# State steps of layer 2: half of the output sum on TensorE, and a new order of rows, experts and softplus parts

## The chip, the cores and the metric

The kernel runs on one core of a Trainium2 chip. The metric is the device time of one execution in microseconds (us). Every time below is in us unless ns is written.

## The reference, cut to what matters

The program is a network of four layers on activations of B = 4 batches, S = 512 positions and D = 128 channels. The change lies in layer 2, which has two parts that work on the same input.

The first is a selective state-space scan with 256 inner channels and 16 states. For every batch the normed input goes through an input projection, a convolution of width 3 and silu, which give x; small products of x give a step size dt (through softplus), and the rows B and C. For every state n of 16 the layer then computes

```
h_t = exp(dt_t * A_n) * h_(t-1) + dt_t * x_t * B_t[n]      (over the 512 positions)
y_t = sum over n of h_t * C_t[n]   (+ D_param * x_t)
```

The sum y is multiplied by silu(z), goes through an output projection, is added to the normed input and normed again.

The second part is a mixture of 8 experts with 512 hidden units each, of which the router chooses two for each position. The silu of its sum gates the first part's result.

## The kernel before, in words

The 256 inner channels lie as two halves m = 0, 1 of 128 partitions each, with the 512 positions along the free axis. A **state step** k (0 to 63) is one state n = k % 16 of one batch b = k // 16; the text says "step 7" for n = 7 of any batch. All five engines run hand-ordered lists of these steps, each in its own `@block`, and signal each other by semaphores. For one step:

- VectorE (loop at L2116 and on): `scan(k)` (L2042) runs the recurrence over 1024 elements; `outs(k-1)` (L2050) multiplies the states of the step before by the row C, one instruction per half; `inputs(k+2)` (L2035) makes dt * x * B for two steps ahead; in even steps `add_expert` (L2066) adds one expert's output, four instructions.
- TensorE (loop at L1814): two `chunk`s (each 4 products of hidden units with `we2`, 16 instructions for both), then `c_row(k)` (the row C of state k copied onto 128 partitions, bank 2; it waits for `outs(k-1)`), two `hidden`s (a 128x128 product of 512 columns each), then `b_row(k+3)` (the row B, bank 1; it waits for `inputs(k+2)`). A product of fp32 operands shows as two instructions; the rows, which are in another type, as one. All matrix products have line L415, a helper's.
- ScalarE (loop at L1952): in even steps the decays exp(dt * A) of two steps (L1915), in odd steps four silus of hidden units (L1903). It loads an activation table each time that it changes between the two.
- GpSimd: `add_y(k)` (L1681) adds the two halves of `outs(k)` to the sum YY (L1693); at a batch's first state it sets each half of YY to D_param * x before (L1689).

H, the buffer of states, has four slots, so `inputs(k)` waits until `add_y(k-4)` is through.

Into these steps the rest of a batch is laid, by hand. The products that use bank 0 ("spares", `spare_at`, L1610 to L1625) are written by TensorE in a fixed order and each waits until the one before is read: the experts' biases in step 1, the output projection `wo` of the batch before in step 3, and for the batch to come the transposes in step 4, the router in 5 and its logits in 6, the convolution `c` (two halves, six instructions each) in 7, `dbc` in 8, `dt` in 9, the transposed weights in 14; `z` in 12 and 13. The first spare of a step stands right behind `c_row`, further ones behind the `hidden`s.

VectorE reads some of them: `biases` (L2055) in step 2, behind `inputs`; `out_stats` (L2080) in step 3, `choose` (L1989 and on) in step 6, `split` (L2006) in step 9, all behind `inputs`. The softplus of the next batch's dt is spread: ScalarE's `dt_parts` in step 9, `dt_exp` (L1876) and `dt_log` (L1882) in step 10; VectorE's `correction` (L2013) in step 10, `share` (L1999) and `dt_sums` (L2020) in step 11, `dt_x` (L2027) in step 13. `gated` (L2073, sum times silu(z)) comes in step 1 of the next batch behind `scan`; ScalarE's `gate` (L1896) comes at the end of its step 1, and `finish` (L2092 and on) in VectorE's step 5.

Of the kernel before, what the change touches and what calls it, by code (L numbers as in the profile page):

```python
# [20 lines left out]
ALU = mybir.AluOpType  # L21
# [3 lines left out]
P = 128  # L25
# [8 lines left out]
def build(nc, I, out):  # L34
    ctx = ExitStack()
    with ctx:
# [1548 lines left out]
        def layer2():  # L1585
# [6 lines left out]
            bm, ex, scn, hc, ya = (lsem(f"a2_{k}") for k in ("inputs", "decays", "scans", "outs", "y"))  # L1592
# [37 lines left out]
            with ExitStack() as c:  # L1630
# [5 lines left out]
                YY = sbr("YY", [P, 2, S], c=c)  # L1636
# [19 lines left out]
                with nc.Block() as block:  # L1656
# [5 lines left out]
                    def _(g):  # L1662
# [18 lines left out]
                        def add_y(k):  # L1681
                            b, n = divmod(k, NS)
                            if n == 0:
                                g.wait_ge(m0, read("c", b, 1))
                                if b:
                                    g.wait_ge(yz, b)
                            for m in range(2):
                                if n == 0:
                                    plink(nc.gpsimd.tensor_scalar(YY[:, m, :], XM[:, m, :], Dp[:, m:m + 1], None, ALU.mult))  # L1689
                                else:  # L1690
                                    g.wait_ge(ya, 2 * k + m - 1)
                                g.wait_ge(hc, 2 * k + m + 1)
                                nc.gpsimd.tensor_tensor(YY[:, m, :], YY[:, m, :], H[:, k % 4, m, :], ALU.add).then_inc(ya, 1)  # L1693

                        nc.gpsimd.memset(XT[:, :, 0:1], 0.0)
                        nc.gpsimd.memset(XT[:, :, S + 1:S + 2], 0.0).then_inc(zd, 1)
                        nc.gpsimd.memset(BCR[0:32, :, :].bitcast(F32), 0.0).then_inc(zd, 1)
                        scales(0)
# [13 lines left out]
                    def _(pe):  # L1712
                        def spare(key):
# [32 lines left out]
                            elif kind == "bias":  # L1746
                                for t in range(T):
                                    last = mm(o[:, t * P:(t + 1) * P], WGT[0:NE, t * P:(t + 1) * P], be2f[0:NE, :])
                            elif kind == "z":
                                last = mm(o, WinT[:, 2 + key[2], :], xt)  # L1750
                            elif kind == "wo":
                                pe.wait_ge(yz, b + 1)
                                for t in range(T):
                                    for m in range(2):
                                        last = mm(o[:, t * P:(t + 1) * P], ZS[:, m, t * P:(t + 1) * P], WoutT[:, m, :],
                                                  start=m == 0, stop=m == 1)
# [11 lines left out]
                        def chunk(g):  # L1768
# [3 lines left out]
                            if i == 0 and j >= 2:  # L1772
                                pe.wait_ge(ad, j - 1)
                            for t in range(T):
                                last = mm(PS[:, 6 + j % 2, t * P:(t + 1) * P], HH[:, i, t * P:(t + 1) * P],
# [14 lines left out]
                        def c_row(k):  # L1790
                            b, n = divmod(k, NS)
                            if k:
                                pe.wait_ge(hc, 2 * k)
                            mm(PS[:, 2, :], SEL[:, NS + n:NS + n + 1].to_broadcast([96, P]), BCR[:, b % 2, :]).then_inc(cp, 1)

# [18 lines left out]
                        for k in range(NK):  # L1814
                            for i in range(2):
                                chunk(2 * k + i)
                            if k:
                                c_row(k)
                            for key in spare_at[k][:1]:
# [6 lines left out]
                            if k + 3 < NK:  # L1826
                                b_row(k + 3)
# [3 lines left out]
                    def _(act):  # L1831
# [24 lines left out]
                        def x_silu(b, m):  # L1856
                            act.wait_ge(mp, read("c", b, m))
                            if b:
                                act.wait_ge(ya, 2 * NS * (b - 1) + 2)
# [20 lines left out]
                        def dt_log(b):  # L1880
                            act.wait_ge(cor, b + 1)
                            nc.scalar.activation(E, E, ACT.Ln, bias=1.0).then_inc(dtl, 1)  # L1882

# [21 lines left out]
                        def decays(k):  # L1905
# [3 lines left out]
                            if k == 0:  # L1909
                                act.wait_ge(wj, 2)  # L1910
                                act.wait_ge(zd, 3)
# [19 lines left out]
                        dt_log(0)  # L1931
                        decays(0)
                        decays(1)
                        store_wT(0)
                        for k in range(NK):
# [14 lines left out]
                            if n == 1 and b:  # L1950
                                gate(b - 1)
                            if n == 3 and more:  # L1952
# [13 lines left out]
                            if n == 10 and more:  # L1966
                                dt_exp(b + 1)
                                dt_log(b + 1)
# [8 lines left out]
                    def _(v):  # L1977
# [51 lines left out]
                        def inputs(k):  # L2029
# [3 lines left out]
                            if k >= 4:  # L2033
                                v.wait_ge(ya, 2 * (k - 3))
# [10 lines left out]
                        def outs(k):  # L2045
                            v.wait_ge(cp, k + 1)
                            v.wait_ge(scn, k + 1)
                            for m in range(2):
                                h = H[:, k % 4, m, :]
                                nc.vector.tensor_tensor(h, h, PS[:, 2, :], ALU.mult).then_inc(hc, 1)  # L2050
# [7 lines left out]
                        def add_expert(j):  # L2058
# [6 lines left out]
                            for t in range(T):  # L2065
                                last = nc.vector.scalar_tensor_tensor(ACC[:, t, :], PS[:, 6 + j % 2, t * P:(t + 1) * P],  # L2066
# [3 lines left out]
                        def gated(b):  # L2070
                            v.wait_ge(m0, read("z", b, 1))
                            v.wait_ge(ya, 2 * NS * (b + 1))
                            nc.vector.tensor_tensor(ZS, ZS, YY[:, :, :], ALU.mult).then_inc(yz, 1)  # L2073
# [39 lines left out]
                        for k in range(NK):  # L2113
# [3 lines left out]
                            if n == 1 and b:  # L2117
                                gated(b - 1)
                            if k:
# [5 lines left out]
                            if n == 2:  # L2125
                                biases(b)
                            if n % 2 == 0 and k:
                                add_expert(k // 2 - 1)
# [8 lines left out]
                            if n == 10 and more:  # L2137
                                correction(b + 1)
                            if n == 11 and more:
                                share(b + 1)  # L2140
                                dt_sums(b + 1)
# [749 lines left out]
```

## Time and profile before

| what | us |
| --- | --- |
| median of 3 runs (lowest, highest) | 1602.43 (1601.49, 1605.38) |
| the profiled execution's own time | 1599.87 |
| its span, first to last instruction | 1596.9 |
| layer 2's state steps, first to last scan start | 893.6 to 1331.0 |
| busy over the span: TensorE, VectorE, ScalarE, GpSimd | 1243.1, 1031.2, 736.3, 617.0 |
| mean granted share of TensorE's clock | 0.891 |

The page divides the span among engines (PE is TensorE, PEld its weight loads, DVE VectorE, ACT ScalarE, POOL GpSimd). The shares are means over layers with different limits, so for this change the views are restricted to 893 to 1335 us, the state steps. A row's last part in square brackets, or behind the last bar, is the idle time of the engine in front of the instruction and the instruction that ended it. PEclk is the granted share of TensorE's clock, 1.00 for 2.4 GHz and 0.5 for 1.2 GHz.

### The profile page before, as it was taken

The page shows a single profiled execution, that of the slowest core. Times are in us where ns is not written, and L with a number is a line of the kernel's source. Part 1 is how long each engine was busy: PE and PEld are TensorE (multiplying, and loading weights), DVE is VectorE, ACT ScalarE, POOL GpSimd, SP SyncE. Part 2 cuts the span into 40 slices and gives each one's busy share as a digit, 9 for nine tenths or more (in the row PEclk, how much of TensorE's full clock was granted, in tenths as well). Part 3 has the DMA queues.
Part 4 walks back from the last instruction along what each step waited for, and adds up shares of the span by engine and source line. Part 5 has one row for each costly group of instructions (what it writes and reads, how often), then busy time and mean ns, then how long its engine had stood idle before and what let it go on. Part 6 is the DMA issues. An engine that isn't in the chain of part 4 may idle for free. (4 is left out here: it accounts for less than half of the span.)

```text
span 1596.9 us, 21351 instructions
## 1 busy us (share of the span) xinstructions
PE 1243.1 (78%) x7092; PEld 834.7 (52%) x7092; DVE 1031.2 (65%) x2384; ACT 736.3 (46%) x1557; POOL 617.0 (39%) x609
## 2 busy tenths in 40 slices
PE   0799999998997776365677687887787774989995
PEld 0345565564464566254554455545545553766664
DVE  1266767668787444356653888988888997634444
ACT  0345555545544335133333667657557572343332
POOL 1243344344338722323311433633633543225551
PEclk9999999999999778577777798999999997699998
DMA  7300000000000112430000000000000000001113
GB/s 168 91 0 2 1 1 1 1 1 1 1 1 27 47 54 85 133 112 21 14 1 11 0 1 1 1 0 1 1 1 1 0 1 0 27 14 36 37 34 91
DMA packets 54457, 40.73 MB, mean 26 GB/s; under 512 B 13191, under 2 KB 46701, under 8 KB 54349
## 3 DMA queue, kind: packets, MB, share of 16 engines
q1 hardware_dynamic: 35660, 24.30, 5.2%
q0 software_dynamic: 4544, 9.32, 2.1%
q10 hardware_dynamic: 14146, 5.75, 1.7%
q8 instruction: 59, 0.97, 0.3%
q14 instruction: 48, 0.39, 0.1%
HBM read 26.32 MB, written 13.04 MB: 25 GB/s over the span
## 5 line engine op out<-in xcount | busy, mean ns | idle before, releaser
L762 POOL TENSOR_TENSOR PR<-PR,R 128x256 f32<-128x256 f32 (+3 forms) x128 | 161.1, 1259 | 269.8 <-DVE R L1216 265.1
L1693 POOL TENSOR_TENSOR YY<-YY,H 128x512 f32<-128x512 f32 x128 | 163.2, 1296 | 244.2 <-DVE H L2050 243.6
L2042 DVE TENSOR_TENSOR_SCAN H<-DA,H 128x1024 f32<-128x1024 f32 x64 | 159.4, 2490 | 0.2
L415 PE MATMUL banks<-BCR,SEL 96*128 96x512 f32 x128 | 89.2, 698 | 88.4 <-DVE H L2050 77.2
L1033 ACT ACTIVATE PR<-banks,NM 128x129 f32<-128x129 f32 (+3 forms) x256 | 132.7, 527 | 44.5 <-DVE NM L1193 43.6
L415 PE MATMUL banks<-XT,we 128*128 128x512 f32 x256 | 139.9, 667 | 11.9 <-ACT HH L1903 11.9
L415 PEld LDWEIGHTS banks<-we,HH 128*128 128x128 f32 x1024 | 131.9, 201 | 20.8 <-issue 17.7
L415 PE MATMUL banks<-we,HH 128*128 128x128 f32 x1024 | 130.9, 283 | 0.0
L1903 ACT ACTIVATE HH<-banks,be1f 128x512 f32<-128x512 f32 x128 | 84.3, 686 | 94.9 <-PE banks L415 94.1
L415 PEld LDWEIGHTS banks<-PTS,V 128*64 128x64 f32 x1280 | 72.7, 143 | 98.7 <-issue 89.1
L415 PE MATMUL banks<-PTS,V 128*64 128x128 f32 x1280 | 104.9, 295 | 15.9 <-DVE PTS L1201 9.7
L1201 DVE COPY PTS<-banks 128x128 f32<-128x128 f32 (+3 forms) x128 | 62.2, 486 | 79.7 <-PE banks L903 78.7
L903 PE MATMUL banks<-ident,PR 128*128 128x128 f32 x640 | 102.9, 294 | 10.2 <-POOL PR L762 10.2
L1041 ACT ACTIVATE PTS<-banks 128x128 f32<-128x128 f32 (+3 forms) x128 | 56.5, 441 | 114.3 <-PE banks L903 114.1
L1193 DVE TENSOR_REDUCE NM<-banks 128x2 f32<-128x258 f32 (+3 forms) x128 | 105.7, 826 | 4.4
L415 PE MATMUL banks<-KT,QT 64*128 64x384 f32 (+3 forms) x512 | 105.6, 490 | 1.7 <-ACT PR L1033 0.8
L2035 DVE TENSOR_TENSOR H<-DTX,banks 128x1024 f32<-128x1024 f32 x64 | 77.6, 1213 | 28.3 <-PE banks L415 23.0
L903 PEld LDWEIGHTS banks<-ident,PR 128*128 128x128 f32 x640 | 71.9, 147 | 34.8 <-issue 34.6
L415 PEld LDWEIGHTS banks<-BCR,SEL 96*128 96x128 f32 x128 | 26.2, 206 | 116.1 <-DVE H L2050 85.7
L415 PEld LDWEIGHTS banks<-XT,we 128*128 128x128 f32 x256 | 51.7, 210 | 63.8 <-issue 42.9
L1915 ACT ACTIVATE DA<-DT,Aneg 128x512 f32<-128x512 f32 (+1 forms) x128 | 81.9, 710 | 1.2 <-DVE DT L2022 0.8
L2050 DVE TENSOR_TENSOR H<-H,banks 128x512 f32<-128x512 f32 x128 | 80.5, 668 | 0.6 <-PE banks L415 0.6
(531 smaller groups left out, 2579.0 us busy)
## 6 DMA issues: line engine op xcount, KB each, us to landing
xsort<-zrow SPq DMA_DIRECT2D x1, 3072.0 KB, 13.1
XS<-xsort SPq DMA_DIRECT2D x12, 256.0 KB, 2.8
ysort<-PTS SPq DMA_DIRECT2D x12, 256.0 KB, 2.2
pj_stage<-in_L_ffn_w_proj SPq DMA_DIRECT2D x1, 2048.0 KB, 10.0
we<-in_L_ffn_we SPq DMA_DIRECT2D x1, 2048.0 KB, 10.8
we<-yrows SPq DMA_DIRECT2D x8, 256.0 KB, 5.0
X<-in_L_attn_resid_pre ACTq DMA_DIRECT2D x4, 256.0 KB, 4.6
xrows<-XN SPq DMA_DIRECT2D x4, 256.0 KB, 2.3
```

What stands on the lines that cost most here:

```text
L415: return nc.tensor.matmul(o, l, r, start=start, stop=stop)
L762: nc.gpsimd.tensor_tensor(p, p, R[:, n, :].unsqueeze(2).to_broadcast([P, 2, w]), ALU.mult).then_inc(pn, 1)
L903: last = nc.tensor.transpose(PS[:, 4 + s, k * P:(k + 1) * P], PR0[:, q % 2, s, a:a + P], ident[:, :])
L1033: nc.scalar.activation(PR0[:, q % 2, s, OFF[t]:OFF[t] + w], ps2(n)[:, s, 0:w], ACT.Exp, bias=NM[:, n, s:s + 1], accum_out=L[:, n, s:s + 1] ...
L1193: nc.vector.tensor_reduce(NM[:, n, :], ps2(n)[:, :, 0:(t + 1) * P + more], AX.X, ALU.max, negate=True).then_inc(nm, 1)
L1201: nc.vector.tensor_copy(PTS[:, m % 2, 1, 0:w], PS[:, 5, 0:w]).then_inc(ptB, 1)
L1693: nc.gpsimd.tensor_tensor(YY[:, m, :], YY[:, m, :], H[:, k % 4, m, :], ALU.add).then_inc(ya, 1)
L1903: nc.scalar.activation(HH[:, i, :], PS[:, 3 + g % 3, :], ACT.Silu, bias=be1f[:, j % NE, i:i + 1]).then_inc(hs, 1)
L1915: nc.scalar.activation(DA[:, k % 4, m, m:], DT[:, b % 2, m, m:], ACT.Exp, scale=Aneg[:, m, n:n + 1]).then_inc(ex, 1)
L2035: nc.vector.tensor_tensor(H[:, k % 4, :, :], DTX[:, b % 2, :, :], PS[:, 1, :].unsqueeze(1).to_broadcast([P, 2, S]), ALU.mult).then_inc(bm, 1)
L2042: nc.vector.tensor_tensor_scan(h, DA[:, k % 4, :, :].rearrange("p m s -> p (m s)"), h, 0.0, ALU.mult, ALU.add).then_inc(scn, 1)
L2050: nc.vector.tensor_tensor(h, h, PS[:, 2, :], ALU.mult).then_inc(hc, 1)
```

## The change

The sum over states is split: GpSimd keeps the half m = 0, in a YY of one half. TensorE sums the half m = 1 in bank 6, by a product of `ident` with the states after `outs` in each step (`sum_y`), and at a batch's first state a product of DD = diag(D_param) with x before it. Bank 6 comes from the experts: their `chunk`s now all use bank 7, and wait for the expert before to be added. D_param * x for half 0 is now made by ScalarE (`begin_y`, at the end of its step 1, behind `gate`).

`outs` is one instruction of 1024 elements, `gated` two of 512.

TensorE's step begins with `c_row(k)` and `sum_y(k-1)`, then `chunk`, `b_row(k+3)`, `chunk`, then the spares and `hidden`s as before. VectorE's `add_expert` and `biases` come before `outs` where they came behind `inputs`. ScalarE's `dt_log` goes from step 10 to 12, VectorE's `correction` from 10 to 11 and `dt_sums` from 11 to 12; `share` stays in 11.

The changed lines (indentation cut by 12):

```diff
@@ -1589,7 +1589,7 @@
-bm, ex, scn, hc, ya = (lsem(f"a2_{k}") for k in ("inputs", "decays", "scans", "outs", "y"))
+bm, ex, scn, hc, ya, yc, yi = (lsem(f"a2_{k}") for k in ("inputs", "decays", "scans", "outs", "y_pool", "y_pe", "y_begun"))
@@ -1633,7 +1633,8 @@
-    YY = sbr("YY", [P, 2, S], c=c)
+    YY = sbr("YY", [P, S], c=c)
+    DD = sbr("DD", [P, P], c=c)
@@ -1681,20 +1682,16 @@
-                    g.wait_ge(m0, read("c", b, 1))
-                    if b:
-                        g.wait_ge(yz, b)
-                for m in range(2):
-                    if n == 0:
-                        plink(nc.gpsimd.tensor_scalar(YY[:, m, :], XM[:, m, :], Dp[:, m:m + 1], None, ALU.mult))
-                    else:
-                        g.wait_ge(ya, 2 * k + m - 1)
-                    g.wait_ge(hc, 2 * k + m + 1)
-                    nc.gpsimd.tensor_tensor(YY[:, m, :], YY[:, m, :], H[:, k % 4, m, :], ALU.add).then_inc(ya, 1)
+                    g.wait_ge(yi, b + 1)
+                else:
+                    g.wait_ge(ya, k)
+                g.wait_ge(hc, k + 1)
+                nc.gpsimd.tensor_tensor(YY[:, :], YY[:, :], H[:, k % 4, 0, :], ALU.add).then_inc(ya, 1)
...
+            nc.gpsimd.tensor_scalar(DD[:, :], ident[:, :], Dp[:, 1:2], None, ALU.mult).then_inc(zd, 1)
@@ -1749,7 +1746,7 @@
-                    pe.wait_ge(yz, b + 1)
+                    pe.wait_ge(yz, 2 * b + 2)
@@ -1769,10 +1766,10 @@
-                if i == 0 and j >= 2:
-                    pe.wait_ge(ad, j - 1)
+                if i == 0 and j:
+                    pe.wait_ge(ad, j)
...
-                    last = mm(PS[:, 6 + j % 2, t * P:(t + 1) * P], HH[:, i, t * P:(t + 1) * P],
+                    last = mm(PS[:, 7, t * P:(t + 1) * P], HH[:, i, t * P:(t + 1) * P],
@@ -1790,8 +1787,20 @@
-                    pe.wait_ge(hc, 2 * k)
+                    pe.wait_ge(hc, k)
...
+
+            def sum_y(k):
+                b, n = divmod(k, NS)
+                if n == 0:
+                    pe.wait_ge(m0, read("c", b, 1))
+                    if b:
+                        pe.wait_ge(yz, 2 * b)
+                    else:
+                        pe.wait_ge(zd, 3)
+                    mm(PS[:, 6, :], DD[:, :], XM[:, 1, :], start=True, stop=False)
+                pe.wait_ge(hc, k + 1)
+                mm(PS[:, 6, :], ident[:, :], H[:, k % 4, 1, :], start=False, stop=n == NS - 1).then_inc(yc, 1)
@@ -1812,10 +1821,13 @@
-                for i in range(2):
-                    chunk(2 * k + i)
...
+                    sum_y(k - 1)
+                chunk(2 * k)
+                if k + 3 < NK:
+                    b_row(k + 3)
+                chunk(2 * k + 1)
@@ -1823,8 +1835,7 @@
-                if k + 3 < NK:
-                    b_row(k + 3)
+            sum_y(LAST)
@@ -1856,7 +1867,8 @@
-                    act.wait_ge(ya, 2 * NS * (b - 1) + 2)
+                    act.wait_ge(yi, b)
+                    act.wait_ge(yc, NS * (b - 1) + 1)
@@ -1881,6 +1893,12 @@
+            def begin_y(b):
+                if b:
+                    act.wait_ge(yz, 2 * b - 1)
+                act.wait_ge(m0, read("c", b, 0))
+                nc.scalar.activation(YY[:, :], XM[:, 0, :], ACT.Copy, scale=Dp[:, 0:1]).then_inc(yi, 1)
+
@@ -1908,7 +1926,7 @@
-                    act.wait_ge(zd, 3)
+                    act.wait_ge(zd, 4)
@@ -1929,6 +1947,7 @@
+            begin_y(0)
@@ -1949,6 +1968,7 @@
+                    begin_y(b)
@@ -1965,6 +1985,7 @@
+                if n == 12 and more:
@@ -2031,7 +2052,8 @@
-                    v.wait_ge(ya, 2 * (k - 3))
+                    v.wait_ge(ya, k - 3)
+                    v.wait_ge(yc, k - 3)
@@ -2045,9 +2067,9 @@
-                for m in range(2):
-                    h = H[:, k % 4, m, :]
-                    nc.vector.tensor_tensor(h, h, PS[:, 2, :], ALU.mult).then_inc(hc, 1)
+                h = H[:, k % 4, :, :]
+                nc.vector.tensor_tensor(h, h, PS[:, 2, :].unsqueeze(1).to_broadcast([P, 2, S]),
+                                        ALU.mult).then_inc(hc, 1)
@@ -2063,14 +2085,16 @@
-                    last = nc.vector.scalar_tensor_tensor(ACC[:, t, :], PS[:, 6 + j % 2, t * P:(t + 1) * P],
+                    last = nc.vector.scalar_tensor_tensor(ACC[:, t, :], PS[:, 7, t * P:(t + 1) * P],
...
-                v.wait_ge(ya, 2 * NS * (b + 1))
-                nc.vector.tensor_tensor(ZS, ZS, YY[:, :, :], ALU.mult).then_inc(yz, 1)
+                v.wait_ge(ya, NS * (b + 1))
+                nc.vector.tensor_tensor(ZS[:, 0, :], ZS[:, 0, :], YY[:, :], ALU.mult).then_inc(yz, 1)
+                v.wait_ge(yc, NS * (b + 1))
+                nc.vector.tensor_tensor(ZS[:, 1, :], ZS[:, 1, :], PS[:, 6, :], ALU.mult).then_inc(yz, 1)
@@ -2116,16 +2140,16 @@
+                if n == 2:
+                    biases(b)
+                if n % 2 == 0 and k:
+                    add_expert(k // 2 - 1)
...
-                if n == 2:
-                    biases(b)
-                if n % 2 == 0 and k:
-                    add_expert(k // 2 - 1)
@@ -2134,10 +2158,10 @@
-                if n == 10 and more:
+                if n == 11 and more:
...
-                if n == 11 and more:
...
+                if n == 12 and more:
```

## Rows read from the trace of the kernel before

**Rows 1.** Four stretches: start:end, length, busy PE PEld DVE ACT POOL, PEclk, DMA.

```profile
893.00:1335.00 442.00, 348.93 (x1610) 234.93 (x1607) 392.93 (x537) 282.61 (x387) 196.75 (x156) 0.91 0.00 1
1010.00:1022.00 12.00, 9.56 (x34) 6.57 (x34) 10.22 (x13) 4.13 (x6) 10.08 (x6) 0.72 0.00 0
1057.00:1061.00 4.00, 3.67 (x5) 1.66 (x6) 4.00 (x3) 0.00 (x0) 2.32 (x2) 0.57 0.00 0
1286.00:1331.00 45.00, 36.96 (x192) 26.07 (x192) 45.00 (x53) 30.45 (x41) 21.41 (x18) 1.00 0.00 1
```

**Rows 2.** VectorE's groups, 893 to 1335: count, busy us, mean ns, idle before.

```profile
L2042 DVE TENSOR_TENSOR_SCAN H<-DA,H 128x1024 f32<-128x1024 f32 x64 | 159.4, 2490 | 0.2
L2050 DVE TENSOR_TENSOR H<-H,banks 128x512 f32<-128x512 f32 x126 | 79.2, 668 | 0.0
L2035 DVE TENSOR_TENSOR H<-DTX,banks 128x1024 f32<-128x1024 f32 x63 | 76.4, 1213 | 28.2 <-PE banks L415 23.0 <-POOL YY L1693 5.0
L2066 DVE SCALAR_TENSOR_TENSOR ACC<-banks,WG,ACC 128x128 f32<-128x128 f32 x124 | 34.7, 340 | 0.4
L2027 DVE TENSOR_TENSOR DTX<-DT,XM 128x1024 f32<-128x1024 f32 x3 | 6.2, 2077 | 0.0
...
L1999 DVE TENSOR_TENSOR PR<-PR,OH 128x32 f32<-128x32 f32 x3 | 3.1, 1045 | 0.0
```

**Rows 3.** VectorE's waits, 893 to 1335: us in total, times, longest.

```profile
DVE H L2035 <- PE banks L415: 23.0, 7, 4.8
DVE DTX L2013 <- ACT EW L1876: 10.7, 3, 3.6
DVE H L2035 <- POOL YY L1693: 5.0, 3, 1.7
DVE XN L2080 <- PE banks L415: 5.0, 3, 2.5
DVE XN L2092 <- ACT XN L1843: 3.5, 3, 1.2
```

**Rows 4.** Timeline of a plain step pair: start us, us, engine, operation.

```profile
1301.61 1.25 DVE L2050 TENSOR_TENSOR H<-H,banks 128x512 f32<-128x512 f32 x2
1302.41 2.50 POOL L1693 TENSOR_TENSOR YY<-YY,H 128x512 f32<-128x512 f32 x2 [3.03 <-DVE H L2050]
1302.78 1.21 DVE L2035 TENSOR_TENSOR H<-DTX,banks 128x1024 f32<-128x1024 f32 x1
...
1302.91 0.50 PE L415 MATMUL banks<-BCR,SEL 96*128 96x512 f32 x1 [1.30 <-DVE H L2050]
...
1303.25 1.88 PE L415 MATMUL banks<-XT,we 128*128 128x512 f32 x4
...
1303.92 3.14 DVE L2042 TENSOR_TENSOR_SCAN H<-DA,H 128x1024 f32<-128x1024 f32 x1
...
1305.20 1.95 PE L415 MATMUL banks<-we,HH 128*128 128x128 f32 x16
...
1310.33 2.27 DVE L2042 TENSOR_TENSOR_SCAN H<-DA,H 128x1024 f32<-128x1024 f32 x1
```

**Rows 5.** Timeline of TensorE after a batch's step 0.

```profile
1012.48 0.50 PE L415 MATMUL banks<-BCR,SEL 96*128 96x512 f32 x1 [2.44 <-DVE H L2050]
1012.91 1.87 PE L415 MATMUL banks<-be2f,WGT 8*128 8x128 f32 x8
```

**Rows 6.** Timeline of the end of a step 3, TensorE and VectorE.

```profile
1264.04 0.50 PE L415 MATMUL banks<-BCR,SEL 96*128 96x512 f32 x1 [2.21 <-DVE H L2050]
...
1264.37 1.95 PE L415 MATMUL banks<-WoutT,SA 128*128 128x128 f32 x16
...
1266.36 0.69 DVE L2080 TENSOR_TENSOR XN<-banks,XN 128x512 f32<-128x512 f32 x1 [1.25 <-PE banks L415]
```

**Rows 7.** Timeline of TensorE in a step 6.

```profile
1049.72 0.95 PE L415 MATMUL banks<-rw,XNT 128*128 128x8 f32 x8
```

**Rows 8.** Timeline of ScalarE in a step 1.

```profile
1019.12 0.62 ACT L1896 ACTIVATE SA<-ACC 128x512 f32<-128x512 f32 x1
```


## Prediction

> **What bounds the kernel now.** The change touches only layer 2's state steps, so I first took busy time by stretch. From 893 to 1335 us VectorE is busy 392.9 of 442 us, TensorE 348.9, ScalarE 282.6, GpSimd 196.8 [rows 1]. VectorE is nearly full there and is the engine to beat. Its groups [rows 2] say what it does and its waits [rows 3] what it lacks: 47.2 us in 21 waits, of which 23.0 are `inputs` waiting for TensorE's row B, 10.7 the softplus, 5.0 GpSimd's sum, 5.0 `out_stats` waiting for the output projection, 3.5 `finish`. 392.9 and 47.2 make up the stretch. So a part of the change counts if it makes VectorE's work shorter or one of its waits shorter or longer. Nothing else does.
>
> The timeline of a plain pair [rows 4] gives the prices. `outs` to `inputs` starts 1.17 apart, `inputs` to scan 1.14. The scan behind `inputs` takes 3.14, the other 2.27: GpSimd's two adds run from 1302.41 to 1304.91, 0.99 into the slow one, and it is 0.87 longer. In an even step the expert stands between and hides that. TensorE starts 0.13 behind the end of `outs`; `c_row` takes 0.34 to the next start; four hidden instructions and `b_row` 1.95, which is 0.43 per fp32 instruction of 512 columns and 0.24 for a row; two `chunk`s 1.95 with the last one's tail, 0.9 each to the next start. That is 4.2 of work in a step of about 5.4, at granted clock 1.00.
>
> **VectorE's own work.** `outs` as one instruction: two take 1.25, and `inputs`, of the same size and with an operand in PSUM, takes 1.21 [rows 2, 4]: -0.04 in 64 steps, -2.5. `gated` in two halves: nothing, it writes the same elements.
>
> GpSimd has one add per step instead of two. It now starts 0.13 behind the whole `outs` and runs 1.27 (half of 2.50), so it ends 1.40 behind `outs`, while `inputs` covers 1.14 and the expert no longer stands behind `inputs`. The scan is met for some 0.3 in nearly every step, where now it is met for 0.99 in a quarter of them. No row has so short a meeting; from 0.87 lost of 0.99, I charge 0.2. Some 38 steps have nothing else in front of the scan: 7.6. Today's excess is 64 x (2.49 - 2.28) = 13.4 [rows 2], so -5.8. Bounds: no loss at all (-13.4) and 0.3 in all 64 (+5.8). `dt_x` at 2.08 against 1.21 and the 32-element product of `share` at 1.05, nearly all of it waiting, meet the same adds [rows 2]: 2.6 each, of which I let 0.3 stay: -4.4. Together **-12.7**.
>
> The Trainium skill (SBUF — State Buffer, "SBUF: two separate sides") says more sharply that VectorE with two SBUF inputs and GpSimd lock each other out until the running instruction ends; the 0.87 here agrees, and by that rule the full 0.3 would be lost, which makes the sum 4 us longer.
>
> **TensorE's step.** `sum_y` is an fp32 product of 512 columns, two instructions, 0.86, the same form as a hidden: 4.2 becomes 5.1. VectorE's plain step becomes 1.13 + 1.14 + 2.28 + 0.2 + 0.55 = 5.3, so TensorE still fits, barely. `b_row(k+3)` moves ahead of the spares and hiddens. What nobody wanted soon is now early, and the spares are late: the first began 0.13 + 0.34 = 0.47 behind `outs`; it now begins 0.86 + 0.9 + 0.24 + 0.9 = 2.9 later, at 3.37. The chunks used to run while VectorE scanned, ahead of the wait for `outs`; now they run behind it. Three spares have a reader in VectorE's queue soon after:
>
> - Biases. In step 1 D times x adds 0.86, so they begin at 4.2 and end at 6.1 (1.87 long [rows 5]). VectorE wants them behind `inputs` and a scan, at 3.42, since `biases` moved ahead of `outs`: 2.7 of waiting, none today, four batches: **+10.8**.
> - Output projection. 3.37 + 1.99 [rows 6] = 5.36, wanted at 1.14: 4.2 in three batches, 12.6 against 5.0 today: **+7.6**.
> - Logits. 3.37 + 0.95 [rows 7] = 4.3, wanted at 1.14: 3.2 in three batches, none today: **+9.5**.
>
> VectorE has no slack to win these back: behind each wait it goes on with full work, as in the stretch from 1286, 45.00 busy of 45 [rows 1].
>
> **The expert's place.** It waits for the second chunk, 3.4 to 3.6 behind the `outs` before, and is wanted at 3.4 to 3.6: 0.1 in some 15 even steps, **+1.5**. One bank for the experts costs nothing, since the add comes ahead of the `outs` that releases TensorE.
>
> **D times x on ScalarE.** Its queue in step 1 is four silus, `gate`, `begin_y`. The last hidden ends at 7.8, then silu 0.6, gate 0.62 [rows 8], copy 0.6: 9.8; GpSimd's add behind it ends at 11.2. `inputs` is wanted at 6.2 + 0.7 + 1.05 + 1.13 = 9.1: 2.1 in three batches against 5.0 today: **+1.3**. In the first batch it lies in the gap before the first decays, which wait for VectorE: nothing. The D diagonal on GpSimd lies in its idle start.
>
> **Steps 7 to 12.** Today 22 (of the 23.0, 0.9 is the start) and 10.7 [rows 3]. New, from the end of `outs` in step 7: TensorE's step is 5.0 + twelve convolution instructions 5.2, ending at 10.3. VectorE comes to step 9's `outs` at 9.3 and gets `c_row` at 10.7: 1.4. `b_row` follows 2.2 behind `c_row`, `outs` covers 1.15: 1.0. `split` wants `dbc`: a chunk 0.9, four instructions 1.7, ScalarE's copy 0.8, less `inputs` 1.14: 2.2. A late chunk in step 10: 0.4. `correction` one step later gains a step, but ScalarE, which sits behind the late dt products, still owes parts 1.3, table 1.3, four decays 2.6, exp 1.0; about 3.4 is left of today's 3.6. Sum 8.4, three batches 25. This is at 2.4 GHz. The granted clock falls to 1.2 GHz on and off: 0.72 in the stretch behind a VectorE-bound gap, 0.57 in a step 7 [rows 1]. The waits in steps 3 and 6 leave TensorE idle 4 us each ahead of step 7, so I add 2.5 per batch: 33 against 33, **0**. Bounds: 25 and 41.
>
> `finish` waits for ScalarE a little more, as `outs` and GpSimd's queue in step 4 are as before: **+0.6**. The tail behind the last scan saves one GpSimd add, and waits for `sum_y` instead: **-1**.
>
> **Sum**: -12.7 + 10.8 + 7.6 + 9.5 + 1.5 + 1.3 + 0 + 0.6 - 1 = **+17.6**. The profiled execution took 1599.9, so it would take 1617.5. The median of the runs shown is 2.6 above it; I give the time against the median: 1602.4 + 17.6 = **1620**.
>
> **Rivals.**
> *Faster.* The waits in steps 7 to 12 are today's largest, and they go because `b_row` no longer stands behind the convolution. For it: 23.0 of them are put on exactly that row [rows 3]. Against: TensorE has 10.2 + 6.8 + 6.8 of work in steps 7 to 9 and VectorE about 18, so the lateness passes on to `c_row` and `split`. If all 33 went: 1587. It decides from 17.6 of the 33. Chance 0.10.
> *No change.* Behind each late spare TensorE has caught up, and part of the 28 of new spare waits is taken off waits that follow; with half of it left, 1606. Against: what follows steps 2, 3 and 6 today is VectorE's own work. Chance 0.14.
> *TensorE at 1.2 GHz where it is waited for.* In steps 3 and 6 its work up to the spare's end is 5.2 and 4.2 and would double, 28 in three batches; in half the cases 14, and 2 more in each step 7: +20, 1640. For it: the new idle gaps. Against: no drop from 1286 to 1331, at 82% busy [rows 1]. Chance 0.16.
>
> The Trainium skill (TensorE: Matmul & The Clock Gate, "HAM oscillation — how this bites in real kernels") warns that work that comes in bursts with waits between them starts each burst at the low clock, which by itself is this third rival; the 0.72 agrees, the 1.00 of the dense stretch too.
>
> My forecast, 1610 to 1632, has 0.60. The range takes the clock bound (-8) with the scan's (-8), and upward the third rival: **1603 to 1638**. About 0.3%, 4.8 us, is what a measurement of this kernel can tell from no change. Slower by more: 0.60, 0.16 and a little of the second rival, 0.78; within it 0.12; faster 0.10.
>
> **What the profile should show.** `biases`, `choose` and `out_stats` waiting for TensorE by about 2.7, 3.2 and 4.2 each time; the scan's mean at about 2.4 with hardly any at 3.1; the wait on GpSimd in step 2 at about 2; `inputs` waiting for `b_row` far less than 23.0, with waits of `outs` and `split` in its place; TensorE busy 50 to 60 more. VectorE's waits in the stretch should come to 77 or so, its work to 380. I am wrong if the biases and logits are there in time, or if waits of steps 7 to 12 fall under 16.

## The result, and the profile after

The changed kernel takes 1635.1 us, median of 4 runs (1633.9 to 1636.0); the kernel before 1603.8 in the 4 runs beside them. The ratio is 1.0196, 95% interval 1.0178 to 1.0214: some 31 us slower. The forecast was 1620, 1603 to 1638: slower, and inside the range, but with 14 more slowdown than the sum had.

The profiled execution has a span of 1633.0 against 1596.9. The page of the changed kernel, part 1:

```profile
PE 1291.5 (79%) x7228; PEld 854.5 (52%) x7228; DVE 1017.0 (62%) x2324; ACT 739.7 (45%) x1561; POOL 519.3 (32%) x538
```

VectorE has 14 us less to do in the whole kernel, TensorE 48 more. The busy times of two stretches of the changed kernel, in the columns of [rows 1]; the first is the state steps to the end of the last scan, the second follows a long wait of TensorE in a step 1:

```profile
893.00:1366.00 473.00, 393.90 (x1718) 253.63 (x1717) 377.98 (x477) 285.30 (x390) 101.13 (x86) 0.93 0.00 1
...
1026.00:1035.00 9.00, 6.05 (x22) 4.56 (x23) 8.86 (x18) 5.48 (x7) 5.98 (x6) 0.62 0.01 3
```

The first answers to the 442 us of [rows 1]: 31.0 longer, while VectorE's work fell from 392.9 to 378.0. So its idle time rose from 49 to 95. Its waits say by what. The waits of the changed kernel's VectorE from 893 to 1375 (us in total, times, longest), which answer to [rows 3]:

```profile
DVE XN L2104 <- PE banks L415: 19.9, 4, 6.5
DVE ACC L2077 <- ACT SA L1914: 15.9, 3, 5.3
DVE ACC L2088 <- PE banks L415: 14.4, 12, 2.9
DVE LG L2010 <- PE banks L415: 9.4, 3, 3.1
DVE H L2071 <- PE banks L415: 8.6, 7, 2.1
DVE DTX L2034 <- ACT EW L1888: 8.0, 3, 2.7
DVE BCR L2027 <- ACT XNT L1877: 6.0, 3, 2.0
DVE H L2057 <- PE banks L415: 5.5, 7, 0.9
DVE XN L2116 <- ACT XN L1854: 3.7, 3, 1.2
DVE DT L2043 <- ACT EW L1894: 3.1, 3, 1.0
DVE ACC L2077 <- PE banks L415: 3.0, 1, 3.0
```

`inputs` (now L2057) waits 5.5 for the row B, not 23.0, and VectorE waits for GpSimd no more. In their place stand the output projection (L2104), the biases (L2077, which wait for ScalarE's `gate`, L1914, in three batches and for their product in the first), the experts (L2088), the logits (L2010), `outs` (L2071) and `split` (L2027).

From the first to the last scan's start the steps took 437.4 before and take 470.2 now, 32.8 more. This length is used below beside the medians, since it leaves the rest of the program out: the rest (span less that length) is 1159.5 before and 1162.8 after, and between 1158 and 1170 in the kernels below. None of them changes anything there but the few us behind the last scan, so a difference of the medians that is not in this length is not put down to an edit.

### The profile page after: what moved, and what is told of

The parts are those of the page before. It is cut to its first block and busy times, and to the rows that moved or that the text cites. A ratio compares the mean times of both kernels' runs of the same rounds, so it can differ in the third digit from the quotient of the medians.

```text
span 1633.0 us, 21503 instructions
## 1 busy us (share of the span) xinstructions
PE 1291.5 (79%) x7228; PEld 854.5 (52%) x7228; DVE 1017.0 (62%) x2324; ACT 739.7 (45%) x1561; POOL 519.3 (32%) x538
## 5 line engine op out<-in xcount | busy, mean ns | idle before, releaser
L1689 POOL TENSOR_TENSOR YY<-YY,H 128x512 f32<-128x512 f32 x64 | 83.5, 1305 | 403.6 <-DVE H L2071 362.5
L415 PEld LDWEIGHTS banks<-we,HH 128*128 128x128 f32 x1024 | 149.2, 210 | 39.9 <-issue 36.5
L2064 DVE TENSOR_TENSOR_SCAN H<-DA,H 128x1024 f32<-128x1024 f32 x64 | 154.4, 2412 | 0.2
L415 PE MATMUL banks<-we,HH 128*128 128x128 f32 x1024 | 147.7, 292 | 0.0
L415 PE MATMUL banks<-BCR,SEL 96*128 96x512 f32 x128 | 76.5, 600 | 81.5 <-DVE H L2071 69.4
L415 PE MATMUL banks<-XT,we 128*128 128x512 f32 x256 | 123.9, 601 | 9.0 <-ACT HH L1921 9.0
L2071 DVE TENSOR_TENSOR H<-H,banks 128x1024 f32<-128x1024 f32 x64 | 77.0, 1203 | 8.6 <-PE banks L415 8.6
L2057 DVE TENSOR_TENSOR H<-DTX,banks 128x1024 f32<-128x1024 f32 x64 | 77.6, 1212 | 5.6 <-PE banks L415 5.5
L415 PE MATMUL banks<-H,ident 128*128 128x512 f32 x128 | 75.5, 675 | 0.0
## 6 DMA issues: line engine op xcount, KB each, us to landing
xsort<-zrow SPq DMA_DIRECT2D x1, 3072.0 KB, 13.1
```

The costliest lines, as they stand in the source:

```text
L415: return nc.tensor.matmul(o, l, r, start=start, stop=stop)
L1689: nc.gpsimd.tensor_tensor(YY[:, :], YY[:, :], H[:, k % 4, 0, :], ALU.add).then_inc(ya, 1)
L2057: nc.vector.tensor_tensor(H[:, k % 4, :, :], DTX[:, b % 2, :, :], PS[:, 1, :].unsqueeze(1).to_broadcast([P, 2, S]), ALU.mult).then_inc(bm, 1)
L2064: nc.vector.tensor_tensor_scan(h, DA[:, k % 4, :, :].rearrange("p m s -> p (m s)"), h, 0.0, ALU.mult, ALU.add).then_inc(scn, 1)
L2071: nc.vector.tensor_tensor(h, h, PS[:, 2, :].unsqueeze(1).to_broadcast([P, 2, S]), ALU.mult).then_inc(hc, 1)
```

## The experiments

All run times are medians. The kernel before was run beside each set: 1603.9, 1604.4 and 1603.5 in the three sets.

### The spares that VectorE reads soon, earlier

```diff
+early = k % NS in (1, 3, 6)
 c_row(k)
+for key in spare_at[k][:early]:
+    spare(key)
 sum_y(k - 1)
...
-for key in spare_at[k][:1]:
+for key in spare_at[k][int(early):1]:
```

> The changed kernel, but the first spare of steps 1, 3 and 6 (the experts' biases, the output projection, the logits) stands right behind c_row, ahead of sum_y and the chunks. Theory A, late spares: out_stats waits 1.3 instead of about 6 in each of three batches, choose not at all instead of 3.1, biases of the first batch not at all instead of 3.0; the 5.3 of biases in the other batches stays, since it is a wait for ScalarE's gate. That is 26 less than the changed kernel: about 1609. Theory B, TensorE has too much work at too low a clock: the same work still has to be done, the waits only move on into c_row and the hiddens, under 8 less: 1627 or more.

1618.6, ratio to before 1.0103 (1.0074 to 1.0133): 16.5 less than the changed kernel. State steps 456.3. The logits' wait is 2.2 in all instead of 9.4, the first batch's for the biases is gone, the output projection's is 11.8 instead of 19.9, the gate's stays at 15.9. Nearer to theory A than to B, with 10 less than it promised: `outs` waits 13.1 for `c_row` instead of 8.6, so a part did only move on.

### TensorE's step in the old order

```diff
-c_row(k); sum_y(k - 1); chunk(2 * k); b_row(k + 3); chunk(2 * k + 1)
+chunk(2 * k); chunk(2 * k + 1); c_row(k); sum_y(k - 1)
 (first spare, hiddens, further spares)
+b_row(k + 3)
```

> The changed kernel with TensorE's step in the order of before (two chunks, c_row, sum_y, first spare, hiddens, further spares, b_row). Theory A: spares are in time (logits without a wait, output projection 2 to 3 per batch), experts wait less, but b_row is late again in steps 7 to 9, about 6 per batch as in the kernel before: about 1612. Theory B: the order does not matter, 1630 to 1640.

1607.6, ratio 1.0024 (1.0014 to 1.0034): 27.5 less than the changed kernel. State steps 443.4. The order of TensorE's step alone thus carries most of the 31, and the time is near theory A's 1612. The waits are not as theory A has them. The logits still wait 7.7, where it had none, and `inputs` waits far more for the row B than in the kernel before, 38.7 against 23.0, some 11 per batch in steps 8 to 10 instead of 6:

```profile
DVE H L2057 <- PE banks L415: 38.7, 19, 5.3
```

The gate's wait is 9.8 instead of 15.9, the first batch's for the biases 0.6, the output projection's 11.2.

### Most of TensorE's sum left out

```diff
-mm(PS[:, 6, :], ident[:, :], H[:, k % 4, 1, :], ...)
+w = S if n in (0, NS - 1) else 8
+mm(PS[:, 6, 0:w], ident[:, :], H[:, k % 4, 1, 0:w], ...)
```

> The changed kernel, but TensorE's product that adds the state to the sum has 8 columns instead of 512 except in states 0 and 15: most of the sum over states of half 1 is left out. It takes some 0.75 per step off TensorE and changes no order and no wait. Theory A (the place of spares, chunks and rows behind outs): about seven waits per batch get 0.75 shorter, 20 less, about 1615. Theory B (the added work of TensorE and its clock are the whole cost): 30 less, 1605 or under. If the work is hidden: 1633.

1630.6, ratio 1.0160 (1.0135 to 1.0186): 4.5 less, where both theories had 20 or more. State steps 468.1 against 470.2. The stretch of state steps in this kernel, in the columns of [rows 1]:

```profile
893.00:1364.00 471.00, 382.34 (x1723) 268.69 (x1722) 377.30 (x476) 283.85 (x390) 100.74 (x86) 0.87 0.00 1
```

56 products of 0.86 were cut to 0.14 each, some 40 us of full-clock work, and TensorE's busy time fell by 11.6: the granted clock is 0.87 over the stretch instead of 0.93. What was taken off came back as work at 1.2 GHz. The logits' wait even grew, from 9.4 to 10.7. So neither theory's account of the product holds. The third case of the expectation, hidden work and 1633, comes nearest: in this order of steps, TensorE's added work costs next to nothing net.

### VectorE's step in the old order

```diff
 scan(k)
-biases(b) (step 2); add_expert(k // 2 - 1) (even steps)
 outs(k - 1); inputs(k + 2)
+biases(b) (step 2); add_expert(k // 2 - 1) (even steps)
```

> The changed kernel with VectorE's biases and add_expert behind inputs again, as before. Theory A: the experts' 14.4 of waits nearly go, since the chunks get 2.3 more time; the biases' wait for the gate gets 2.3 shorter in three batches; in even steps the expert again stands between inputs and the scan, so that the scan meets GpSimd in half of the steps only (some 5 less). Against it some of the same lateness comes back in c_row and b_row in steps 8 to 10: 18 less in all, about 1617. If the place of the experts does not matter, since TensorE is late anyway: 1630 to 1637.

1626.9, ratio 1.0147 (1.0127 to 1.0167): 8.2 less, half of what was expected. The experts' wait is 1.4 and the median scan 2.281, as expected. But `outs` waits 20.3 for `c_row` (8.6), and `inputs` in step 2 waits 18.7 for GpSimd, up to 6.2 at a time, whose sum begins behind `begin_y`: the gate was only the first of two things that late silus hold up in ScalarE's step 1.

### The softplus part alone, on the kernel before

```diff
-(step 10) dt_exp; dt_log    (VectorE, step 10) correction
+(step 10) dt_exp            (step 11) correction
+(step 12) dt_log
-(VectorE, step 11) share; dt_sums
+(VectorE, step 11) share   (step 12) dt_sums
```

> The kernel before with the softplus part of the change alone: dt_log in step 12, correction in 11, dt_sums in 12. If VectorE's wait for the exponent (10.7 in three batches) is only moved, since ScalarE is as late a step later, no change: 1603. If a step later it is covered: 7 to 10 less, 1595. If the logarithm a step later opens a wait of its own: 3 more.

1590.5, ratio 0.9920 (0.9898 to 0.9942): **13.9 faster than the kernel before**, state steps 425.4. The 10.7 of waiting for the exponent are gone altogether, and `inputs` still waits 23.2 for its row, its only wait in steps 7 to 12 of this kernel:

```profile
DVE H L2036 <- PE banks L415: 23.2, 7, 4.8
```

My sum had this part as worth 0.2 per batch.

### The row B ahead of the spares in steps 7 to 9, on the kernel before

```diff
+late = k % NS in (7, 8, 9)
+if late: b_row(k + 3)
 (first spare, hiddens, further spares)
-b_row(k + 3)
+if not late: b_row(k + 3)
```

> The kernel before with b_row ahead of the first spare in steps 7, 8 and 9 alone. Theory A: of the 22 of waits that inputs has for that row in steps 8 to 10, about half goes and the rest turns into a wait of outs for c_row: 10 less, 1593. Theory C, TensorE's work in steps 7 to 9 is the limit and any order passes the lateness on: no change, 1602 or more.

1612.8, ratio 1.0046 (1.0028 to 1.0064): 8.4 slower. VectorE's waits in this kernel, from 893 to 1350:

```profile
DVE DTX L2016 <- ACT EW L1879: 28.0, 3, 10.0
DVE H L2053 <- PE banks L415: 12.6, 4, 4.5
```

The wait for the row is gone and 12.6 of waiting for `c_row` stand in its place, as in theory A; but the wait for the exponent grew from 10.7 to 28.0. VectorE came sooner to a thing that was ready later. TensorE's rows from step 7's `c_row` to the first half of the convolution (operands XT and WJ) show why, in the kernel before and then in this one:

```profile
1057.33 0.63 PE L415 MATMUL banks<-BCR,SEL 96*128 96x512 f32 x1 [2.81 <-DVE H L2050]
1057.76 4.33 PE L415 MATMUL banks<-XT,WJ 128*128 128x512 f32 x6
```

```profile
1056.79 0.79 PE L415 MATMUL banks<-BCR,SEL 96*128 96x512 f32 x1 [2.82 <-DVE H L2053]
1057.92 0.80 PE L415 MATMUL banks<-BCR,SEL 96*128 96x512 f32 x1 [0.34 <-DVE H L2038]
1058.51 5.08 PE L415 MATMUL banks<-XT,WJ 128*128 128x512 f32 x6
```

The row B now waits for `inputs` and runs ahead of the convolution, which begins 1.4, 1.3 and 1.1 later behind `c_row` in the three batches. From step 7's `c_row` to the second dt product it is 0.2, 3.0 and 3.3 longer, 6.4 together; the state steps are 444.5, 7.1 longer. What the row itself does not explain, 2.6 of the 6.4, are rows at another clock: the convolution above takes 5.08 instead of 4.33, and in the first batch some rows ran faster than before.

### Gate and the start of the sum earlier in ScalarE's step 1

```diff
 for i in range(4):
+    if n == 1 and b and i == 2:
+        gate(b - 1); begin_y(b)
     hidden(2 * k + 2 + i)
-if n == 1 and b:
-    gate(b - 1); begin_y(b)
```

> The changed kernel with only gate and begin_y moved up in ScalarE's step 1, between its second and third silu. If the 5.3 that biases waits in batches 1 to 3 is the gate behind late silus, it shortens to the 3.0 of the first batch, where only the row of biases is late: 7 less, 1628. If the biases' product itself is that late: 1635.

1620.9, ratio 1.0108 (1.0089 to 1.0127): 14.2 less than the changed kernel, twice the 7. The biases' waits are 9.2 in four batches instead of 18.9, all for their product now, 2.1 in batch 1. So the biases gave 9.7, and the output projection one step on gave 5.2: it waits 12.5 in three batches instead of 17.7. That is 4.2 each time, what the prediction had for it with TensorE in time for step 3's `outs`.

### Two orders put together

```diff
 chunk(2 * k); chunk(2 * k + 1); c_row(k)
 (first spare, in steps 1, 3 and 6)
 sum_y(k - 1)
 b_row(k + 3)
 (first spare in other steps, hiddens, further spares)
```

with `gate` and `begin_y` as in the last one, and all else as in the changed kernel.

> The changed kernel (sum split between GpSimd and TensorE, VectorE's and softplus's new places kept) with TensorE's step as: two chunks, c_row, the first spare in steps 1, 3 and 6, sum_y, b_row, first spare in other steps, hiddens, further spares; and with gate and begin_y between the second and third silu of ScalarE's step 1. Theory A: VectorE's work stays near 380 and its waits fall to 40 or less: about 1580. Theory B (TensorE's added product limits in any order): 1600 or more.

1590.0, ratio 0.9899 (0.9876 to 0.9922): faster than the kernel before, by 14, and 45 faster than the changed kernel, but 10 short of theory A's 1580. State steps 421.2. It is no faster than the kernel before with the softplus part alone (1590.5).

The same with `b_row` at the end of TensorE's step, where the kernel before has it:

> As e9_reordered, but b_row at the end of TensorE's step, as in the kernel before. If an early b_row is what the change had right, this is slower than e9_reordered by some 10: 1600. If the early row only turns into a wait of outs for c_row and passes through the softplus, as on the kernel before: the same or faster, 1580 to 1590.

1579.7, ratio 0.9849 (0.9832 to 0.9865): **24 faster than the kernel before and 55 faster than the changed one.** State steps 418.4. It is the fastest kernel here, and the second of the two expectations holds. The stretch of its state steps, in the columns of [rows 1], and then VectorE's waits in layer 2:

```profile
893.00:1312.00 419.00, 372.71 (x1718) 240.96 (x1718) 371.97 (x476) 282.94 (x388) 106.96 (x86) 0.98 0.00 1
```

```profile
DVE H L2060 <- PE banks L415: 32.4, 16, 4.1
...
DVE XN L2107 <- PE banks L415: 6.8, 4, 2.2
...
DVE XN L2119 <- ACT XN L1857: 5.0, 2, 3.8
```

What is left is mostly `inputs` waiting for the row B. TensorE issues as many instructions as in the changed kernel, x1718, in 372.7 of busy time instead of 393.9, because the granted clock is 0.98. The early `b_row` does not help in either kernel. On the kernel before it costs 8.4 by the medians and 7.1 by the state steps. Here it is 10.3 by the medians, but only 2.8 by the state steps of the profiled executions (421.2 and 418.4): the rest of these two executions, where the kernels are the same, differs by 12. So its price here is between 3 and 10, and open.

Of the 24 that this kernel gains on the kernel before, the softplus part alone gives 13.9 there. The rest of the change, with the old row order, the early spares and the early gate, is worth the other 10.8 in all. No run has the early spares or an earlier gate on the kernel before, so whether the split of the sum gains anything is not shown.

### The softplus part taken back out of the change

The edit of the softplus experiment, reversed, on the changed kernel.

> The changed kernel with the softplus part taken back (dt_log in step 10, correction in 10, dt_sums in 11). On the kernel before, that part alone gained 13.9. If it gains the same inside the change: 1649. If TensorE's lateness in steps 8 to 10 has eaten what it gives, so that ScalarE's exponent comes as late as before: 1635 to 1640.

1644.3, ratio 1.0242 (1.0225 to 1.0259): 9.2 more. The wait for the exponent is 26.8 without the part and 8.0 + 3.1 with it. Between the two expectations; the part is worth 9 inside the change and 14 outside.

### The split of the sum alone

The sum on both engines with one bank for the experts; `chunk`, `c_row`, `b_row`, VectorE's step and the softplus as in the kernel before, `sum_y` behind `c_row`.

> The split of the sum alone: TensorE's step, VectorE's step and the softplus in the order of the kernel before, with one bank for the experts and sum_y behind c_row. Its even steps have two chunks that wait for add_expert, which stands behind inputs, ahead of c_row: if that one bank is not hidden, c_row comes 2 late in each even step and TensorE's idle time grows: 1640 or more. If it is hidden: the gain on VectorE (12.7 less) against spares 0.9 later (some 8 more): 1600.

1704.3, ratio 1.0627 (1.0610 to 1.0645), state steps 538.8. TensorE's waits in this kernel, from 893 to 1430:

```profile
PE banks L415 <- DVE ACC L2087: 111.6, 31, 6.4
```

1640 or more was expected if the one bank is not hidden, and it is not. There is a wait in nearly every even step, for that bank: the chunk waits for an expert that VectorE adds at the end of its step, and `c_row` and `b_row` stand behind the chunk in TensorE's queue. On VectorE `inputs` waits 82.2 and `outs` 27.6 for these rows. So the new places of the rows or of the experts are not a choice of their own: with the bank given away, one of them has to move. Moving the experts and the biases in VectorE's step takes most of it away: the kernel with the old TensorE order, 1607.6, differs from this one by that and by the softplus part, which was worth 9 to 14 elsewhere.

### Most of GpSimd's sum left out

The add of half 0 has 8 columns instead of 512, except in states 0 and 15.

> The changed kernel with GpSimd's add of 8 columns instead of 512 except in states 0 and 15: most of the sum over states of half 0 is left out. The scans of 2.51 should go to 2.28, 8.3 less of VectorE's work. If it is on the path in all steps: 1627. If much of it lies in front of a wait for TensorE, which then only grows: about 1630.

1623.3, ratio 1.0108 (1.0089 to 1.0127): 11.9 less than the changed kernel by the medians; the state steps are 462.1 against 470.2, 8.1 less, against 8.3 expected. The scans of the changed kernel and of this one (duration ns min/median/max, first and last start):

```profile
L2064 DVE TENSOR_TENSOR_SCAN H<-DA,H x64: 2256/2510/2986, 893.5 to 1363.7; 128x1024 f32<-128x1024 f32 x64
```

```profile
L2065 DVE TENSOR_TENSOR_SCAN H<-DA,H x64: 2256/2284/2526, 894.2 to 1356.3; 128x1024 f32<-128x1024 f32 x64
```

VectorE is busy 370.0 over the state steps instead of 378.0. The lengthening of the scans is GpSimd's add, and in the changed kernel it is on the path in full.

## Why the prediction was right, and where its size was off

By its own steps, in us over the state steps of the profiled executions:

| term | predicted | measured | from |
| --- | --- | --- | --- |
| VectorE's work | -12.7 | -15.0 | 392.9 to 378.0 |
| biases | +10.8 | +18.9 | 3.0 + 15.9 |
| GpSimd's sum in step 2 | +1.3 | -5.0 | no wait left |
| output projection | +7.6 | +12.7 | 19.9, less 2.2 behind the last scan, less 5.0 |
| logits | +9.5 | +9.4 | 9.4 |
| experts outside steps 8, 10 | +1.5 | +2.6 | 14.4 less 10.4 there and 1.4 at the end |
| steps 7 to 12 | 0 | +7.3 | 40.1 less 32.8 |
| `finish` | +0.6 | +0.2 | 3.7 less 3.5 |
| sum | +18.6 | +31.1 | 442 to 473 is 31.0 |

Behind the last scan 1.7 was gained (from the last `outs` but one to the projection's reader 10.6 before, 9.0 after), where 1 was expected.

Two readings in the prediction are off without a consequence for the sum: [rows 3] has 19 waits, not 21, and 392.9 and 47.2 make 440.1 of the 442, so that 1.9 of short gaps are in neither.

**Right.** The direction and the mechanism: VectorE's work falls, and three spares with near readers, now behind chunk, row and chunk, cost more than that. The logits' term is exact, and an experiment on the place of the spares took 16.5 off. The size was right in part by luck. 1635 lies above the forecast of 1610 to 1632, and inside the range only by the room kept for the third rival; a missing 5.0 for GpSimd's sum made up for part of the biases, and two wrong parts cancelled in steps 7 to 12. The longer scan beside GpSimd: charged 0.2, it is 0.24 in 33 of 64 scans, as this pair of the changed kernel's timeline shows:

```profile
1320.87 1.21 DVE L2057 TENSOR_TENSOR H<-DTX,banks 128x1024 f32<-128x1024 f32 x1
...
1321.10 1.28 POOL L1689 TENSOR_TENSOR YY<-YY,H 128x512 f32<-128x512 f32 x1 [7.83 <-DVE H L2071]
...
1322.01 2.52 DVE L2064 TENSOR_TENSOR_SCAN H<-DA,H 128x1024 f32<-128x1024 f32 x1
```

GpSimd is 0.37 into the scan, and the scan is 0.24 longer than 2.28; in [rows 4] it was 0.99 and 0.87. The loss is the meeting less 0.12 or 0.13 in both, and in the other scans that meet the add for these times. The Trainium skill (SBUF — State Buffer, "SBUF: two separate sides") says that the later of the two is blocked until the running one ends; but for that 0.13 the trace agrees. A loss in proportion to the meeting would be 0.33 here and does not fit.

**The biases.** The step that failed has VectorE wanting them at 3.42 and waiting only for their product, to 6.1. `biases` also waits for ScalarE's `gate` of the batch before (it overwrites the sum that `gate` reads), and `gate` stands behind four silus of which the last two follow the late spare. I priced exactly that queue for `begin_y`, and did not see that `biases` waits on it too. In the kernel before the wait was hidden, since `inputs` waited 1.7 for GpSimd first. The experiment with the gate moved up confirms the wait: it took 9.7 off the biases. So the biases' 5.3 a time took the place of the 2.1 that I had charged to GpSimd's sum; the two terms together are 13.9, against 12.1. The product itself is 1.08 at full clock, not 1.87: [rows 5] fell in a stretch at the low clock.

**The output projection.** The step that failed took TensorE as waiting when step 3's `outs` ended. It was not. These are TensorE's rows in the changed kernel in steps 2 and 3 of a batch:

```profile
1028.95 0.80 PE L415 MATMUL banks<-BCR,SEL 96*128 96x512 f32 x1 [4.44 <-DVE H L2071]
1029.54 1.91 PE L415 MATMUL banks<-H,ident 128*128 128x512 f32 x2
1031.25 1.92 PE L415 MATMUL banks<-we,HH 128*128 128x128 f32 x8
...
1035.66 0.80 PE L415 MATMUL banks<-BCR,SEL 96*128 96x512 f32 x1
1036.30 1.02 PE L415 MATMUL banks<-H,ident 128*128 128x512 f32 x2
```

It idled 4.44 while VectorE waited for the gate; the rows behind it ran at 1.2 GHz (`sum_y` 1.91 for two instructions, 1.02 later; clock 0.62 in that stretch); and step 3's `c_row` began 1.1 behind the end of `outs` instead of 0.13. The idle time and the low clock that VectorE's wait had made came back as the next wait. The experiment with the gate moved up shows it: with 1.2 of idle time in place of the 4.4 the projection waits 4.2 each time, as predicted, instead of 5.5 to 6.5. That is the third rival, at a part of its price. The Trainium skill (TensorE: Matmul & The Clock Gate, "HAM oscillation — how this bites in real kernels") describes bursts that start slow behind each wait; these rows agree.

**Steps 7 to 12.** The lateness of `c_row` (2.0), `b_row` (0.8), `split` (2.0) in steps 8 and 9 came as worked out (1.4, 1.0, 2.2). What was missed is the expert in step 8. Its second chunk was taken as ready at 3.4 to 3.6, and TensorE, which had idled 4.1 in front of step 7, ran from `c_row` to the chunk at half speed. TensorE's rows, and then the expert's row on VectorE:

```profile
1071.88 0.80 PE L415 MATMUL banks<-BCR,SEL 96*128 96x512 f32 x1 [4.08 <-DVE H L2071]
1072.47 1.91 PE L415 MATMUL banks<-H,ident 128*128 128x512 f32 x2
1074.17 1.91 PE L415 MATMUL banks<-we,HH 128*128 128x128 f32 x8
1075.74 0.77 PE L415 MATMUL banks<-BCR,SEL 96*128 96x512 f32 x1
1076.31 1.81 PE L415 MATMUL banks<-we,HH 128*128 128x128 f32 x8
```

```profile
1078.16 1.12 DVE L2088 SCALAR_TENSOR_TENSOR ACC<-banks,WG,ACC 128x128 f32<-128x128 f32 x4 [2.77 <-PE banks L415]
```

This wait is 2.5, 2.8 and 2.9 in the three batches, 8.1 together, a little more than the whole miss of 7.3. A wait of `outs` in step 11, 0.6 a time, was not in the sum either. I had put 2.5 per batch for the clock, but into one sum of 33 whose upper bound, 41, is what came.

Inside that sum two parts were wrong and, as far as the experiments on single parts show, cancelled. I took the softplus part as worth nearly nothing; it gains 9 to 14. And I took `inputs`' 22 of waiting for the row B as nearly all won by the early `b_row`, with some 11 of waiting for `c_row` and `split` in return; alone, on the kernel before, the early row costs 7 to 8. What the runs showed in its place: in steps 7 to 10 the end is set by the chain convolution, `dbc`, dt products on TensorE, then parts, table, decays and exponent on ScalarE. VectorE's waits for `b_row` stand in front of its wait for the exponent and cover it. Take them away and the later one grows (10.7 to 28.0); move the later reader by a step and it goes. The early row also makes the chain itself longer, by the 6.4 worked out in its experiment, of which 3.8 is the row in front of the convolution. How much of the rest is a lower clock that the edit brought, and how much its chance from run to run, is not shown.

**The rivals.** *Faster* named the right waits, since 23.0 for the row did fall to 5.5, but not that they cover others. *No change* held that waits behind the late spares would shrink by half of the 28. They did not: biases, projection and logits came to 46.0, and steps 7 to 12 grew as well. *TensorE at 1.2 GHz where it is waited for* came in part: 5.1 more than worked out in step 3 (17.7 for 12.6), nothing in step 6, 8.1 at the expert behind step 7, where it had 28 for steps 3 and 6 and 2 for each step 7. TensorE's added work is not the cause by its amount: leaving most of the product out won 4.5.

**Still open** is the exact share of the clock in the 31: no run changes the clock alone, and every kernel that removes the gaps also removes waits.

## What to carry to other kernels

Before moving an instruction behind others in a queue, list for every reader the time from its trigger to its need, and all semaphores that the reader waits for, also those that another wait hides today. On a saturated engine a wait in front of another may only cover it: test the last reader of the chain first, here by moving it one step later (14 us gained by that alone, more than half of what the fastest kernel gains), and only then shorten the waits in front of it. Put what is read within the same step first in a queue and what is read a step later last; the same work so ordered, with `gate` moved up, was 55 us faster than the change.

## What the runs showed of the hardware that was not expected

Cutting some 40 us of TensorE's full-clock work left its busy time 11.6 shorter and the kernel 4.5 faster, as the granted clock fell from 0.93 to 0.87 over the state steps. And the same 1718 instructions were busy for 393.9 at 0.93 and for 372.7 at 0.98.

A scan of 128x1024 that begins while GpSimd's add runs is longer by the rest of the add less 0.12 or 0.13: 0.87 longer at 0.99, 0.24 at 0.37. With most of the add left out the median scan fell from 2.510 to 2.284 us.
